# Selective state-space layer with routed experts on one core: state sums as wide identity products, output projection in halves, reordered prologue and sends

## What is computed

```
xp, res = split(x @ W_in.T)                 # 512 + 512 channels
xc = silu(causal_conv4(xp) + conv_b)
B, C, dt = split(xc @ W_x.T)                # 16 + 16 + 1
dt = softplus(dt @ W_dt.T + b_dt)           # 512 channels
h[t] = exp(A * dt[t]) * h[t-1] + dt[t] * B[t] * xc[t]     # for each of 16 states
y = silu(sum over states of h * C + D * xc + res) @ W_out.T
x = layernorm(x + y)
x = layernorm(x + sum over the two best experts of weight * (gelu(x @ w1.T + b1) @ w2.T + b2))
```

## Time and profile before

| | |
|---|---|
| median of 3 runs | 1610.7 us |
| the profiled execution | 1612.57 us, span of its instructions 1611.0 us |
| mean granted TensorE clock | 0.912 |
| PE, weight loads, DVE, ACT, POOL busy | 83%, 69%, 72%, 65%, 66% of the span |
| first scan starts | 61.5 us |
| last scan ends | 995.7 us |
| first product of the experts' phase | 1076 us |

### The profile page before, as it was taken

How to read it: one execution, slowest core, us unless ns; L and a number is a source line. 1 busy time by engine, 2 the same in 40 slices (tenths; PEclk the granted TensorE clock), 3 DMA queues, 4 the chain that set the end, 5 groups by cost and what they waited for, 6 DMA issues and landing times. The chain is left out here.

```text
span 1611.0 us, 29240 instructions
## 1 busy us (share of the span) xinstructions
PE 1336.9 (83%) x8770; PEld 1118.7 (69%) x8771; DVE 1157.4 (72%) x2036; ACT 1041.1 (65%) x1438; POOL 1059.9 (66%) x989
## 2 busy tenths in 40 slices
PE   3598898898798898798887796639999999999970
PEld 1367577576577576576577685439999999999970
DVE  2678888888888888888888687436666666666646
ACT  3798996996996996996996874413333333333334
POOL 0288878778877978877978888344444444444436
PEclk8699899999999899999899798659999999999995
DMA  2032132222222222222212223441343631511108
GB/s 98 14 99 80 63 105 76 76 80 89 92 77 89 85 84 89 92 78 88 89 67 85 90 85 122 131 129 53 107 133 117 199 121 39 160 39 40 33 26 308
DMA packets 85677, 150.12 MB, mean 93 GB/s; under 512 B 11408, under 2 KB 34576, under 8 KB 85584
## 3 DMA queue, kind: packets, MB, share of 16 engines
q1 hardware_dynamic: 70480, 116.91, 22.7%
q0 software_dynamic: 9888, 27.29, 5.1%
q10 hardware_dynamic: 5216, 4.74, 0.9%
HBM read 104.45 MB, written 44.45 MB: 92 GB/s over the span
## 5 line engine op out<-in xcount | busy, mean ns | idle before, releaser
L1019 POOL TENSOR_TENSOR arena<-arena 128x1024 f32<-128x1024 f32 x256 | 611.2, 2394 | 73.0 <-DVE arena L796 61.9
L397 PEld LDWEIGHTS d_ps<-ident,arena 128*128 128x128 f32 x2048 | 257.4, 150 | 203.0 <-DVE arena L796 101.5
L397 PE MATMUL d_ps<-ident,arena 128*128 128x128 f32 x2048 | 337.7, 291 | 73.0 <-DVE arena L796 67.5
L618 ACT ACTIVATE arena<-u_tok,b_tok 128x512 f32<-128x512 f32 x512 | 327.3, 713 | 74.4 <-PE d_ps L397 72.8
L796 DVE TENSOR_TENSOR_SCAN arena<-arena,carry,d_ps 128x512 f32<-128x512 f32 x256 | 320.6, 1271 | 74.2 <-PE d_ps L397 72.9
L796 DVE TENSOR_TENSOR_SCAN arena<-arena,d_ps 128x512 f32<-128x512 f32 x256 | 305.1, 1211 | 79.4 <-PE d_ps L397 67.6
L410 PE MATMUL y_ps<-ident,arena 128*128 128x128 f32 x2048 | 311.0, 282 | 40.6 <-POOL arena L1019 40.6
L410 PEld LDWEIGHTS y_ps<-ident,arena 128*128 128x128 f32 x2048 | 248.7, 147 | 47.3 <-POOL arena L1019 47.3
L1306 ACT ACTIVATE h_t<-ht_ps 128x512 f32<-128x512 f32 x142 | 84.5, 595 | 289.8 <-PE ht_ps L1361 289.8
L629 ACT ACTIVATE arena<-dt,neg_a 128x2048 f32<-128x2048 f32 x128 | 255.4, 1995 | 1.9 <-DVE arena L796 1.3
L1371 PEld LDWEIGHTS y_ps<-arena,h_parts 128*128 128x128 f32 x1704 | 214.4, 192 | 8.8 <-issue 4.0
(11 more groups left out here) (170 smaller groups left out, 1681.9 us busy)
## 6 DMA issues: line engine op xcount, KB each, us to landing
arena<-c_rows SPq DMA_DIRECT2D x128, 256.0 KB, 3.4
weight_parts<-arena SPq DMA_DIRECT2D x80, 256.0 KB, 3.8
arena<-weight_parts SPq DMA_DIRECT2D x20, 1024.0 KB, 5.3
arena<-in_pieces SPq DMA_DIRECT2D x80, 128.0 KB, 3.6
xg<-expert_rows POOLq DMA_DIRECT2D x71, 130.0 KB, 2.4
arena<-expert_out SPq DMA_DIRECT2D x16, 512.0 KB, 10.4
arena<-in_pieces SPq DMA_DIRECT2D x12, 512.0 KB, 7.2
x_t<-in_x_t SPq DMA_DIRECT2D x8, 512.0 KB, 5.5
```

The lines of the kernel that those rows point to most:

```text
L397: last = nc.tensor.matmul(d_ps[:, c % 2, j * P:(j + 1) * P], ub[:, g % U_RING, j, c * P:(c + 1) * P], t.ident[:], start=True, stop=True, i ...
L618: nc.scalar.activation(ub[:, g % U_RING, j, :], u_tok[:, j, :], ACT.Identity, scale=b_tok[:, b % 2, j, n:n + 1]).then_inc(scaled, 1)
L1019: nc.gpsimd.tensor_tensor(h[:, g % H_RING, lo:hi, :], h[:, g % H_RING, lo:hi, :], c_row[:, g % C_RING:g % C_RING + 1, :].broadcast_to([P, ...
```

## The change

The sum over states stays in state layout. `sum_states` issues for each quarter one product of 128x128 (the identity, stationary) by 128x512 (h, moving), without `is_transpose`; `y_ps` has channels on partitions, and so have gate and skip. `y_silu` then gives what the output projection needs as it is: `turn_y` and `yt_out` are gone with their places. `y_silu` runs in two halves of the tokens, and out0 waits for the first half only, out1 for the second; out0 stands in steps 4 to 6, out1 in 8 and 9, residual at (7, 0) and (10, 0), rstds at 10, normed at 11. `y_u` and `tmp` become `u` and `ys`.

The sends are one in each of steps 10 to 13 and two in steps 14 and 15. Expert 7's weights are split in the prologue in four big parts that lie in the ring of h (casts on ACT, differences on POOL, loads and stores on SP; the first scan waits for the stores), so that a block has 8 pieces instead of 10. In the prologue half of w_in is loaded first and x on ACT's queue; ACT has an order of its own for iterations -2 and -1; for block 0 DVE makes the linear part of the time steps from a second bank (`first_sizes`), and the first scaled inputs are read from PSUM (`first_scale`). `soft_tail` moves from step 7 to 8, `add_sizes` to (9, 3) and (10, 2), `inputs` to (11, 1) and (11, 3). The one-hot rows of the router are one instruction instead of eight. After the last block own_high and own_low stand in steps 3 to 10 instead of 6 to 13.

```diff
-BANK_OF = {"turn0": 0, "turn1": 1, "logits": 0, "ssm": 1, "yt0": 0, "yt1": 0, "z": 1, "yt2": 0, "yt3": 0,
-           "out0": 0, "ranks": 1, "out1": 1, "btok": 0, "in0": 0, "in1": 1, "ut0": 0, "ut1": 1, "ut2": 0, "ut3": 1,
-           "in2": 0, "in3": 1}
+BANK_OF = {"turn0": 0, "turn1": 1, "logits": 0, "ssm": 1, "out0": 0, "z": 1, "z2": 2, "ranks": 1, "btok": 0,
+           "out1": 1, "in0": 0, "in1": 1, "ut0": 0, "ut1": 1, "ut2": 0, "ut3": 1, "in2": 0, "in3": 1}
...
-        PIECE_STEPS = (0, 1, 3, 4, 6, 8, 9, 10, 11, 12)
-        PARTED = (EXPERTS - W_RING) * PIECES
+        PIECE_STEPS = (0, 1, 3, 4, 6, 8, 10, 12)
+        PARTED = (EXPERTS - W_RING - 1) * PIECES
...
                 def sum_states(b, k):
...
-                    for j in (2 * (q % 2), 2 * (q % 2) + 1):
-                        for c in (2 * half, 2 * half + 1):
-                            last = nc.tensor.matmul(y_ps[:, j, c * P:(c + 1) * P],
-                                                    h[:, g % H_RING, c, j * P:(j + 1) * P], t.ident[:],
-                                                    start=(n == 0 and c == 0), stop=(n == STATE - 1 and c == EC - 1),
-                                                    is_transpose=True)
-                    if q == 3:
+                    last = nc.tensor.matmul(y_ps[:, c, :], t.ident[:], h[:, g % H_RING, c, :],
+                                            start=(n == 0), stop=(n == STATE - 1))
+                    if c == 3:
                         last.then_inc(sum_done, 1)
...
-                def skip(j):
-                    for c in range(EC):
-                        nc.tensor.matmul(y_ps[:, j, c * P:(c + 1) * P], xc[:, i % 2, c, j * P:(j + 1) * P],
-                                         t.diag_d[:, c, :], start=False, stop=False)
+                def skip(c):
+                    nc.tensor.matmul(y_ps[:, c, :], t.diag_d[:, c, :], xc[:, i % 2, c, :], start=False, stop=False)
...
-                        gates = ((4, 2), (4, 3), (5, 1), (5, 2), (5, 3), (6, 0), (6, 2), (6, 3))
+                        gates = ((4, 0), (4, 3), (5, 2), (6, 1), (6, 3), (7, 1), (7, 2), (7, 3))
...
-                        skips = ((10, 2), (12, 0), (13, 0), (13, 2))
+                        skips = ((10, 2), (11, 0), (12, 2), (13, 1))
...
-                    if back and n in (9, 10):
-                        m = 4 * (n - 9) + q
+                    if back and n in (8, 9):
+                        m = 4 * (n - 8) + q
                         out_projection(1, m, m + 1)
...
                 def y_silu():
                     act.wait_ge(sum_done, STATE * (r + 1))
-                    nc.scalar.activation(y_u[:], y_ps[:], ACT.Silu).then_inc(ys_done, 1)
+                    if r >= 1:
+                        wait_filled(act, "out1", r - 1)
+                    for lo in (0, T // 2):
+                        nc.scalar.activation(ys[:, :, lo:lo + T // 2], y_ps[:, :, lo:lo + T // 2], ACT.Silu)\
+                            .then_inc(ys_done, 1)
...
-                        if n >= 12:
-                            send_rows(p, n - 12)
+                        if n >= 10:
+                            send_rows(p, n - 10)
+                        if n >= 14:
+                            send_rows(p, n - 8)
```

More of the change, by code:

```diff
@@ L34 @@
 W_LOADS = 4
-FIRST_LOADS, TAP_LOADS, REST_LOADS = 2, 2, 8
+FIRST_LOADS, TAP_LOADS, REST_LOADS = 2, 2, 9
 W_RING = 3
@@ L258, in mamba @@
         w_low = sem("w_low")
+        first_raw = [sem(f"first_raw{m}") for m in range(4)]
+        first_high = sem("first_high")
+        first_low = sem("first_low")
+        first_stored = sem("first_stored")
         high_done = sem("high_done")
@@ L726, in router_exp @@
                     nc.scalar.activation(ex[:], ex[:], ACT.Exp).then_inc(ex_done, 1)
+                if i == -2:
+                    for c in range(EC):
+                        xp_out(c)
+                    for m in range(FIRST_PARTS - 1):
+                        first_part(m)
+                    return
+                if i == -1:
+                    silu()
+                    act.wait_ge(t.rest_loaded, 16 * REST_LOADS)
+                    first_part(3)
+                    ssm_out()
+                    for c in range(EC):
+                        z_parts(c)
+                    soft_tail()
+                    nc.scalar.activation(t.neg_a[:], t.neg_a[:], ACT.Exp).then_inc(exp_done, 1)
+                    decays(0)
+                    xp_out(0)
+                    xp_out(1)
+                    wait_freed(act, "btok", 0)
+                    for j in range(TT):
+                        first_scale(j)
+                    for j in range(TT):
+                        ut_out(j)
+                    for j in range(TT):
+                        wait_freed(act, f"ut{j}", 0)
+                    scale(1)
+                    decays(1)
+                    xp_out(2)
+                    xp_out(3)
+                    return
                 for n in range(STATE):
@@ L753, in step @@
                         turned_out(1)
-                    if back and n == 3:
-                        yt_out(0)
-                    if back and n == 4:
-                        yt_out(1)
+                    if place and n == 4:
+                        router_exp()
                     if front and n in (5, 6):
@@ L760, in step @@
                         z_parts(2 * n - 9)
-                    if back and n in (5, 6):
-                        yt_out(n - 3)
-                    if place and n == 5:
-                        router_exp()
                     if front and n == 9:
@@ L768, in step @@
                         xp_out(n - 11)
+                    if back and n == 11:
+                        normed()
                     if front and n == 13:
@@ L771, in step @@
                         ut_out(1)
-                    if back and n == 14:
-                        normed()
                     if early and n == 15:
```

228 lines of the change are left out of this document (134 added, 94 removed).

## The result

The changed kernel takes 1647.4 us (median of 4 runs, 1644.0 to 1653.3) against 1610.0 us before (4 runs): 1.0236 of its time, 95% interval 1.0202 to 1.027. It is 37.3 us slower, where +12.7 was forecast. The sign was right and the time lies in the range, but two thirds of the loss were not in the sum. The profiled execution took 1653.31 us, the slowest of the four.

The account below looks back on a forecast made before the run. No engine bounds the whole span; PE bounds steps 4 to 8. Prologue and block 0 -1, block 1 +7.1, blocks 2 to 6 +20.0, block 7 +1.4, tail -14.8: +12.7, 1623.5 us against 1610.7, range 1597 to 1653.

Parts of the forecast that it names:

- The sign: Whole kernel: the change makes it slower, chance 0.66.
- The price of the change: State sums: each of 64 quarter sums a block costs PE 0.42 us more, +26.9 us a block.
- 124.3 was forecast: Blocks 2 to 6: each takes 124.3 us against 120.3, +20.0 us for the five.
- the 1.7 us ahead: Steps 4 to 8: PE does 1.7 us ahead while DVE ends step 3, so the stage takes 41.6 us.
- not 31.0: Steps 12 to 15: PE's 30.3 us plus 0.7 for step 13 give 31.0 us, against 26.1.
- The reason given for steps 0 to 3: Steps 0 to 3: earlier sends and fewer pieces end POOL's backlog, helping shorten the stage from 30.5 to 25.3 us.
- Rival (c): Steps 0 to 3 do not shorten, as ACT's silus hold them: +5.2 us in six blocks, 1655 us; chance 0.15.
- rival (a): Blocks 2 to 6: the wide products fit in PE's idle time, blocks stay at 120.3, 1597 us; chance 0.20.
- 24 + 87 = 111: Block 7: without front work it takes 111 us against 109.6, +1.4.
- 31.9 becomes 20: Tail from y_silu on: 31.9 us becomes 20, -12 of the tail's -14.8.
- Prologue with blocks 0 and 1: Start of the kernel: -1 us for prologue and block 0, +7.1 for block 1, +6.1 together.
- not near 50: Prologue: the first scan comes at about 50 us instead of 61.5.

Follow-up runs that it names:

- e4: Changed kernel with the casts and differences of the own expert weights back in steps 6 to 13 after the last block; 1649.3 us.
- e6: Changed kernel with its row sends again two per step in steps 12 to 15, as before the change; 1644.8 us.
- e2: Kernel before, with only each quarter sum's four transposes replaced by one wide product, output not the reference's; 1690.4 us.
- e1: Changed kernel with each wide product of the state sum replaced by four transposes, output not the reference's; 1574.8 us.
- e12: Changed kernel with every second quarter sum by a wide product and the others by four transposes; 1594.2 us.
- e8: Changed kernel, but in the tail VectorE does the router's ranks ahead of the first residual, not behind it; 1644.5 us.
- e9: Changed kernel with sums, gates, skips, turns, y_silu, output projection, residuals, variance and norm as in the kernel before; 1575.5 us.
- e7: Changed kernel, but in the tail the load of x_tok is issued on SP ahead of own-weight loads 4 to 11; 1651.8 us.

## Why the prediction went wrong

Of the 28.0 us that the profiled executions lost beyond the sum (+40.7 against +12.7), 8.5 are in the tail, 7.5 in block 7, 7.7 in blocks 2 to 6 (some 6 of them the clock's) and 4.3 in the prologue with blocks 0 and 1. The price of the change held; the two terms of the sum that failed by most are block 7 and the tail.

**The price, and the blocks between.** "+0.42 each, +26.9 us of PE work" held, row by row. The busy time of PE grew by 22.7 us a block ((608.99 - 495.30) / 5). It is less than 26.9, in part because busy time counts 0.60 us for four transposes with idle time behind them and 0.44 where the next record follows. Of the stages, in e4, whose step 2 was granted 0.78 to 0.90 in these blocks and not 0.50, blocks 2 to 5 take 125.6 to 126.2 us where 124.3 was forecast: steps 4 to 8 take 43.4 and not 41.6, as PE never got the 1.7 us ahead that I subtracted (in the changed kernel's block 4 the stage starts at 579.27 and its first sum at 579.07), and steps 12 to 15 take 29.7 to 29.9 and not 31.0. Block 6 takes 119.1, since it has no in-projection for a block two ahead, which I overlooked. The five together come to 622.2 us for 621.5: right as a sum by luck, since the longer blocks 2 to 5 (+5.9) and the shorter block 6 (-5.2) cancel.

**The reason given for steps 0 to 3 was not needed.** They shortened, as said. The cause named was the sooner sends and fewer pieces; e6 puts the sends back and the stage stays short (25.85 us a block), and e2 shortens it with no other edit (27.36). The wide products alone do it; so does the rest alone (27.75 in e1), and together they give less than their sum. Rival (c) fell, as the stage did shorten, and rival (a), that they fit in PE's idle time, is true of half of them in blocks 2 to 6 (e12) and false of all.

**Block 7, +1.4 forecast, +8.9 measured**, is one step that failed: "24 + 87 = 111". The 24 for steps 0 to 3 has no working in the prediction, which names only PE's work for this block. They take 28.47 us, with PE busy 20.63 (window of the changed kernel):

```profile
924.27:952.74 28.47, 20.63 (x103) 13.91 (x102) 22.18 (x33) 25.87 (x32) 26.14 (x17) 0.82 0.25 84
```

POOL is busy 26.14 of them, and in the first two steps PE waits for it, 2.6 us in all (order of time on PE):

```profile
933.45 1.13 PE L432 MATMUL y_ps<-arena,ident 128*128 128x512 f32 x2 [2.21 <-POOL arena L1082]
```

POOL brings work over from block 6, whose last steps have two sends each and no in-projection to slow PE down; that this is what lets the backlog return here alone was argued from the trace, not tried. The sends' place is not it: e6, with two a step from step 12 on, takes 27.12 us there. What brings the stage to 28.47 therefore stays open. The other 3 us are in steps 4 to 15: 90.1 where 87 was counted, with PE busy in all of it, so there the count of PE's work was short.

**The tail, -14.8 forecast, -6.3 measured**, is the other, and its failing step is "31.9 becomes 20": it became 27.7. The part up to y_silu went by the forecast (-3.7 for -2.8). In the other I subtracted turn_y, yt_out and half a silu from the length without asking what the sooner projection would meet. It met a load behind the own weights on SP's queue, and a VectorE order in which the bank that PE needs is freed behind the residual that waits for this load. That the casts of steps 3 to 10 were to blame is not borne out: e4 moved them and the wait stayed. In the kernel before, the turns and copies covered the load: it was issued at 1017.0, landed in 8.8 us, and the first residual, at 1031.7, waited for PE. And router_rank stood ahead of that residual, with its `base` at 1027.6; the change put it behind. e8, which undoes only this order, gives back 3.8 of the 7.7 us; the other half stays open, and so do 1.6 us that the changed kernel takes longer behind the norm.

**Prologue with blocks 0 and 1, +6.1 forecast, +10.4 measured.** The first scan came at 54.5, not near 50. The order of time on PE shows what I left out:

```profile
45.71 3.65 PE L497 MATMUL y_ps<-ident,u 128*128 128x128 f32 x16 [3.57 <-DVE u L883]
49.15 4.90 PE L456 MATMUL m_ps<-x_t,w_in 128*128 128x512 f32 x8
53.89 1.04 PE L421 MATMUL d_ps<-ident,arena 128*128 128x128 f32 x8
```

The turns of u, at a granted clock of 0.50, and then the second half of the next block's in-projection, at 0.73, stand on PE ahead of the first drive. They took 3.65 and 4.90 us; in the kernel before, at a granted clock of 1.00, 1.91 and 3.62. The sum had only gains on ACT and DVE, and no term for PE. Step 4 came at 81.2 for 79 and block 1 took 123.2 for 121.0; neither was tried by an experiment.

**The clock** gives the rest, some 6 us of the profiled execution by my estimate above (629.14 against e8's 622.73); the sum had no term for it.

## What to carry to other kernels

Price a change of one engine's work by the slack of each stage, not by its sum: in the middle blocks the first half of the added work filled TensorE's waits and was nearly free, at 94% busy in the end, the second half cost most of its length, and with all of it another gain (18 us from the sends) was worth nothing. When two ideas come in one change, measure each in the absence of the other; the fastest version here that computes the whole layer (e9) keeps the small moves and leaves out the wide products and the state layout. And where a stretch at the end loses a stage, look for the load and for the in-order neighbours that the lost stage had covered, before its length is subtracted.

## What the runs showed that was not expected

- Twelve loads of 512 KB issued back to back held SP's queue for 16.1 us (21.1 in the kernel before), and the load issued behind them landed after 9.7 us where its median was 4.7. With eight of these loads behind it instead, its issue took 0.34 us instead of 1.62.
- The mean granted clock over the span, with PE's busy share of it, was 0.912 before (83%), 0.925 in e9 (85%), 0.937 in e12 (88%) and 0.940 in the changed kernel (91%). The two don't go together throughout: e1 has 0.926 at 83% and e8 0.950 at 90%.
- Executions of kernels that are the same up to the last scan differ in the clock granted in step 2 of some blocks: in blocks 3 and 4 it took 7.82 and 7.70 us in the changed kernel's profiled execution and in e7's, at 0.50, and 6.13 and 5.71 in e8's, at 0.76 and 0.80. Only one of the changed kernel's four runs was profiled, so how much of their 9 us of spread this makes is not shown.
